# The final token mix of a gated four-layer kernel, taken one batch at a time

## The reference, cut to what matters

```python
# the last attention (8 heads of 4 channels), then the last feed-forward part
x = x + tanh(g_xattn[3]) * L3_xattn(layernorm(x), ctx, ctx, ...)
xn = layernorm(x)
x_prev = concat([zeros, xn[:, :-1]], axis=1)        # the token before
xr = mu_r * xn + (1 - mu_r) * x_prev
xk = mu_k * xn + (1 - mu_k) * x_prev
r = sigmoid(xr @ W_r.T)                             # receptances
k = square(relu(xk @ W_k.T))                        # gates
x = x + tanh(g_ffn[3]) * (r * (k @ W_v.T))          # values
```

## Time and profile before

| what | value |
|---|---|
| time of three executions | 1080.51, 1083.62, 1086.57 us; median 1083.62 |
| the profiled execution | 1080.08 us |
| its span | 1078.3 us, 17505 instructions |
| PE busy | 985.0 us (91% of the span) |
| DVE busy | 776.8 us (72%) |
| ACT busy | 486.8 us (45%) |
| POOL busy | 290.1 us (27%) |

### The profile page before, as it was taken

The page is one execution under the profiler, slowest core; times in us unless marked ns, Lnnn a source line. Parts: engine busy times, 40 slices in busy tenths (PEclk is TensorE's granted clock), DMA queues, the critical chain, the costliest instruction groups (busy, mean ns, idle before and its releaser), DMA issues.

```text
span 1078.3 us, 17505 instructions
## 1 busy us (share of the span) xinstructions
PE 985.0 (91%) x6556; PEld 582.9 (54%) x6556; DVE 776.8 (72%) x1467; ACT 486.8 (45%) x707; POOL 290.1 (27%) x439
## 2 busy tenths in 40 slices
PE   8888975999999977999689999998889999899988
PEld 4323343544444444999254444455678788644445
DVE  5789978999999632454489999985645654799946
ACT  2463341377777710121027777775212212357742
POOL 3556611133343202002313333331300500023320
PEclk9799986999999977999899999999999999899999
DMA  6689921102430333895331233101354242100011
GB/s 204 224 270 292 364 58 65 43 24 89 128 101 24 91 87 112 306 375 187 92 141 54 60 90 87 46 2 41 99 174 137 98 137 82 28 15 18 2 31 39
DMA packets 79181, 121.81 MB, mean 113 GB/s; under 512 B 9733, under 2 KB 52904, under 8 KB 79090
## 3 DMA queue, kind: packets, MB, share of 16 engines
q1 hardware_dynamic: 59278, 79.29, 23.8%
q10 hardware_dynamic: 19044, 39.22, 10.4%
q0 software_dynamic: 768, 2.10, 0.6%
HBM read 92.10 MB, written 27.81 MB: 111 GB/s over the span
## 4 chain that ended last, share of the span: by engine, by line
PE 70%; DVE 21%; issue 4%; ACT 2%; POOL 2%; DMA 1%; SPq 0%; POOLq 0%; DVEq 0%; ACTq 0%
PE bank L1546 14%; PE bank L1512 14%; PE bank L1737 12%; DVE arena L2229 9%; PE st_bank L1667 4%; PE bank L1679 4%; PE st_bank L1531 3%; PE bank L1314 2%; PE st_bank L1737 2%; PE st_bank L1464 1%; PE bank L1584 1%; PE st_bank L1302 1%; PE bank L1565 1%; DVE bnst L1832 1%; DVE arena L1961 1%
## 5 line engine op out<-in xcount | busy, mean ns | idle before, releaser
L2229 DVE TENSOR_REDUCE arena<-bank 128x1 f32<-128x512 f32 x640 | 397.2, 681 | 34.2 <-PE bank L1512 33.2
L1178 ACT ACTIVATE arena<-st_bank 128x1024 f32<-128x1024 f32 x320 | 312.1, 1022 | 136.1 <-PE st_bank L1531 135.0
L1512 PE MATMUL bank<-g_a 64*128 64x512 f32 x480 | 182.3, 480 | 10.7 <-DVE arena L2229 2.5
L1546 PE MATMUL bank<-arena,vaug 128*9 128x256 f32 (+2 forms) x2560 | 168.5, 381 | 2.0 <-ACT arena L1178 2.0
L1512 PEld LDWEIGHTS bank<-g_a 64*128 64x128 f32 x480 | 73.8, 184 | 123.8 <-DVE arena L2229 99.0
L1737 PE MATMUL bank<-g_a,g_w 128*128 128x512 f32 x512 | 117.7, 390 | 4.3 <-DVE g_w L2460 3.2
L1531 PE MATMUL st_bank<-g_a 64*128 64x512 f32 x480 | 115.2, 417 | 0.0
L1737 PEld LDWEIGHTS bank<-g_a,g_w 128*128 128x128 f32 x512 | 95.8, 188 | 25.5 <-DVE g_w L2460 3.6
L901 POOL COPY arena<-arena 8x32 f32<-8x32 f32 x160 | 34.7, 217 | 257.9 <-issue 137.1
L1546 PEld LDWEIGHTS bank<-arena,vaug 128*9 128x9 f32 (+2 forms) x2560 | 55.8, 92 | 75.7 <-issue 39.1
L1512 PE MATMUL bank<-g_x,g_a 64*128 64x512 f32 x160 | 63.1, 497 | 9.6 <-DVE arena L2229 3.5
(11 more groups left out here) (321 smaller groups left out, 1491.1 us busy)
## 6 DMA issues: line engine op xcount, KB each, us to landing
arena<-in_glu_w SPq DMA_DIRECT2D x39, 512.0 KB, 3.3
arena<-kv_table SPq DMA_DIRECT2D x11, 1024.0 KB, 7.9
ctxT<-in_glu_w ACTq DMA_DIRECT2D x22, 512.0 KB, 6.0
arena<-in_w SPq DMA_DIRECT2D x20, 512.0 KB, 6.3
kparts<-arena ACTq DMA_DIRECT2D x12, 512.0 KB, 5.2
arena<-in_w ACTq DMA_DIRECT2D x12, 512.0 KB, 3.6
xnT<-kv_table SPq DMA_DIRECT2D x5, 1024.0 KB, 7.7
g_a<-kparts SPq DMA_DIRECT2D x24, 192.0 KB
```

What stands on the lines that cost most here:

```text
L1178: act.activation(prob[sl % PROBS], st_bank[sl % 2][:], ACT.Exp, scale=scale).then_inc(exp_ready, 1)
L1512: pe.matmul(bank[TURN_BANKS[place % 3]], Qc[gi % KQ_BUFS][rows, qt * P:(qt + 1) * P], Kc[gi % KQ_BUFS][rows, half * CH:(half + 1) * CH], s ...
L1546: ins = pe.matmul(bank[7][at:at + dh + 1, 0:D], vaug[l][:, b * KT + 2 * m + i, h0 + hh, :], tiles[:, a], start=(m == 0 and i == 0), stop=( ...
L2229: dve.tensor_reduce(mxh[gi % 2][:, col, hf:hf + 1], bank[TURN_BANKS[place % 3]], AX.X, ALU.max).then_inc(max_red, 1)
```

## The change

- `mix_loads` moves in SP's list from the end to the start of the third layer's attention, behind the first group's shift rows; it waits for the x that this attention starts from. The mix's arrays now begin behind the attention's part of the arena, so that they can be filled meanwhile.
- Slots 60 and 61 get a step `mix tokens` each in place of their dummies: the norm's transposes of batch 0, one chunk to a slot, through the rotation's banks. DVE copies them out, and after the second makes xk of batch 0.
- Around the last value products, the last context and heads stand the gate products of batch 0, in halves: `mix` (first half of a chunk's accumulation) and `mix rest` (second half). ACT makes the scaled part of xr for batch 0 at the first, and clips the gates at each second half; DVE squares them, and after the second makes xr of batch 0.
- Behind the attention PE does receptances of batch 0, half of its values, the norm's transposes of batch 1, the other half of the values, gates, receptances and values of batch 1. The dummies there are gone.
- ACT takes the sigmoid of two tiles at a time, and does for batch 1 the scaling by mu straight from the bank. DVE only adds the shifted part, and for batch 0 multiplies and adds two tiles at a time.

The diff, cut: the same edits of names in lists are left out, and so are the removed lines of the final mix on PE and DVE, which stand in the code above.

```diff
@@ -103,11 +103,12 @@
 WEIGHT_SLOTS = (2, 6)
-LN_HOLDS = {3: 8, 4: 16, 7: 16}
+LN_HOLDS = {3: 8, 4: 16}
+MIX_BANKS = {"r": (0, 1), "v0": (2, 3), "k1": (6, 7), "v1": (4, 5, 2, 3)}
 SECOND_TOKENS_AT, SECOND_BANKS = 3, 2
 GATHERED_HOLDS = 19
 QUERY_HOLDS = {1: 10, 2: 4}
-CTX_HOLD, UNIT_HOLD, MIX_HOLD = 14, 44, 22
+CTX_HOLD, UNIT_HOLD = 14, 44
...
@@ -148,6 +149,9 @@
         last = first + EC[l] + 2
         finish[last] = ("variance", b)
         finish[last + NORMAL_LAG] = ("normalise", b)
+        if l == 3:
+            for c in range(DC):
+                finish[last + NORMAL_LAG + 2 + c] = ("mix tokens", (b, c))
     def turn(kind, *what):
...
+            if sl in finish and finish[sl][0] in ("heads", "out", "mix tokens"):
                 turn(*finish[sl])
             elif sl in finish:
                 steps.append(finish[sl])
...
+    def first_gate(c):
+        turn("mix", c)
+    def second_gate(c):
+        steps.append(("mix rest", *next(step[1:] for step in steps if step[:2] == ("mix", c))))
+    if l == 3:
+        first_gate(0)
+    steps += [("values", NGROUPS[l] - 1, m) for m in range((KT - VALUES_LAG + 1) // 2, KT // 2)]
+    if l == 3:
+        second_gate(0)
+    steps.append(("copy", NGROUPS[l] - 1))
     context(NGROUPS[l] - 1)
-    steps.append(("tokens", 0))
+    if l == 3:
+        first_gate(1)
+    else:
+        steps.append(("tokens", 0))
     for c in range(EC[l]):
         turn("heads", (B - 1, c))
+    if l == 3:
+        second_gate(1)
     for i in range(2):
         turn("out", (B - 1, i))
...
+        r = Region(after_att)
         mwr, mwk, mwv = (r.take([DC, D]) for _ in range(3))
...
@@ -746,6 +767,8 @@
                         keys_load(l, g)
                     queries_load(l, g) if g else first_queries(l)
                 shift_load(l, 0)
+                if l == 3:
+                    mix_loads()
                 for g in range(ng):
                     if g + 1 < ng:
                         shift_load(l, g + 1)
@@ -801,7 +824,7 @@
                     glu_chunk_load(sp, n)
             def mix_loads():
-                sp.wait_ge(x_ready, 7 * NT)
+                sp.wait_ge(x_ready, 6 * NT)
                 for dst, n in ((mwr, "w_r"), (mwk, "w_k"), (mwv, "w_v")):
                     ld(dst, rows(io[n]), fin_ld)
...
@@ -1134,6 +1156,11 @@
                 else:
                     ins = act.activation(qph[k % 2][0][0:n], bank[j][0:n], ACT.Identity, bias=w[l]["bq"][:, j % EC[l]:j % EC[l] + 1])
                 ins.then_inc(qp_hi, 1)
+            def clipped(b, c, gates):
+                act.wait_ge(rk_mm, 4 * b + c + 1)
+                act.activation(kact[:, c, b * CH:(b + 1) * CH], gates, ACT.Relu).then_inc(rk_relu, 1)
...
                         act.activation(pvs[gi % 2], bank[7][:, 0:D], ACT.Copy).then_inc(pv_evac, 1)
+                    elif step[0] == "mix" and step[1] == 0:
+                        act.wait_ge(fin_ld, 16 * 5)
+                        act.wait_ge(xnT_ready, LN_AT[7] * 4 + DC)
+                        for c in range(DC):
+                            act.activation(xr[:, c, 0:CH], xnT[:, c, 0:CH], ACT.Copy, scale=mmu[:, 0, c:c + 1]).then_inc(mix_scaled, 1)
+                    elif step[0] == "mix rest":
+                        _, c, place = step
+                        clipped(0, c, bank[TURN_BANKS[place % 3]])
                     elif step[0] == "tokens" and l == 2:
...
-            ln_evac(7)
-            for i in range(B * DC):
-                h, c = i // DC, i % DC
-                act.wait_ge(rk_mm, i + 1)
-                act.activation(kact[:, c, h * CH:(h + 1) * CH], bank[i], ACT.Relu).then_inc(rk_act, 1)
-            for t in range(NT):
-                act.wait_ge(rk_mm, B * DC + t + 1)
-                act.activation(rv[:, t, :], bank[6 + t % 2][:, 0:D], ACT.Sigmoid).then_inc(rk_act, 1)
+            def receptances(b):
+                for i in range(QT // 2):
+                    t = b * QT + 2 * i
+                    act.wait_ge(rk_mm, 4 * b + DC + i + 1)
+                    act.activation(rv[:, t:t + 2, :].rearrange("p t d -> p (t d)"), bank[MIX_BANKS["r"][i]], ACT.Sigmoid).then_inc(rk_act, 1)
+            act.activation(exp_ready_table[:], onesf[0:1, 0:1], ACT.Sigmoid)
+            receptances(0)
+            for c in range(DC):
+                act.wait_ge(xnT_mm, LN_AT[7] * 4 + DC + c + 1)
+                act.activation(xnT[:, c, CH:2 * CH], bank[SECOND_BANKS + DC + c], ACT.Copy).then_inc(xnT_ready, 1)
+                act.activation(xk[:, c, CH:2 * CH], bank[SECOND_BANKS + DC + c], ACT.Copy, scale=mmu[:, 1, c:c + 1]).then_inc(mix_scaled, 1)
+            for c in range(DC):
+                act.activation(xr[:, c, CH:2 * CH], bank[SECOND_BANKS + DC + c], ACT.Copy, scale=mmu[:, 0, c:c + 1]).then_inc(mix_scaled, 1)
+            for c in range(DC):
+                clipped(1, c, bank[MIX_BANKS["k1"][c]])
+            receptances(1)
...
+                    if kind == "mix":
+                        return rk_relu, what + 1
                     if kind == "out":
                         return x_ready, stage * NT + what[0] * QT + what[1] * 2 + 2
...
                     ins.then_inc(ctxT_mm, 1)
+                def mix_tokens(which, place):
+                    b, c = which
+                    pe.wait_ge(*bank_read(place))
+                    for t in range(b * QT, (b + 1) * QT):
+                        pe.wait_ge(xn_ready, XN0[7] + t + 1)
+                        ins = pe.transpose(bank[TURN_BANKS[place % 3]][:, t % QT * P:(t % QT + 1) * P], xn[:, t, c * P:(c + 1) * P], ident[:])
+                    ins.then_inc(xnT_mm, 1)
+                def first_gate(c, i, place):
+                    pe.wait_ge(mix_ready, DC)
+                    if i == 0:
+                        pe.wait_ge(*bank_read(place))
+                    ins = pe.matmul(bank[TURN_BANKS[place % 3]], mwk[:, i, c * P:(c + 1) * P], xk[:, i, 0:CH], start=(i == 0), stop=(i == DC - 1))
+                    if i == DC - 1:
+                        ins.then_inc(rk_mm, 1)
                 def output(which, place):
...
@@ -1796,31 +1866,39 @@
             attention(3)
...
+            def receptances(b):
+                pe.wait_ge(mix_ready, 4 * b + 2 * DC)
+                for i in range(QT // 2):
+                    if b:
+                        pe.wait_ge(rk_act, i + 1)
+                    for t in range(b * QT + 2 * i, b * QT + 2 * i + 2):
+                        for k in range(DC):
+                            ins = pe.matmul(bank[MIX_BANKS["r"][i]][:, t % 2 * D:(t % 2 + 1) * D], xr[:, k, t * P:(t + 1) * P], mwr[:, k, :], start=(k == 0), stop=(k == DC - 1))
+                    ins.then_inc(rk_mm, 1)
+            def mixed_values(b, i):
+                pe.wait_ge(rk_sq, DC * (b + 1))
+                for t in range(b * QT + 2 * i, b * QT + 2 * i + 2):
+                    mixed_v = bank[MIX_BANKS["v1"][t % QT]][:, 0:D] if b else bank[MIX_BANKS["v0"][i]][:, t % 2 * D:(t % 2 + 1) * D]
+                    for k in range(DC):
+                        ins = pe.matmul(mixed_v, kact[:, k, t * P:(t + 1) * P], mwv[:, k, :], start=(k == 0), stop=(k == DC - 1))
+                    ins.then_inc(fv_mm, 1)
+            receptances(0)
+            mixed_values(0, 0)
+            ln_transposes(7, [1], SECOND_BANKS)
+            mixed_values(0, 1)
+            for i in range(DC):
+                pe.wait_ge(mix_ready, 2 * DC + i + 1)
+                for c in range(DC):
+                    ins = pe.matmul(bank[MIX_BANKS["k1"][c]], mwk[:, i, c * P:(c + 1) * P], xk[:, i, CH:2 * CH], start=(i == 0), stop=(i == DC - 1))
+                    if i == DC - 1:
+                        ins.then_inc(rk_mm, 1)
+            receptances(1)
+            pe.wait_ge(xnT_ready, (LN_AT[7] + 1) * 4)
+            pe.wait_ge(mix_scaled, 3 * DC)
+            for i in range(QT // 2):
+                mixed_values(1, i)
...
                 ch.link(ins)
+            def shifted(i, dst, b, c):
+                lo, hi = b * S, (b + 1) * S
+                dve.scalar_tensor_tensor(dst[:, c, lo + 1:hi], xnT[:, c, lo:hi - 1], mom[:, i, c:c + 1], dst[:, c, lo + 1:hi], ALU.mult, ALU.add).then_inc(mix_ready, 1)
+            def squared(b, c):
+                dve.wait_ge(rk_relu, DC * b + c + 1)
+                ka = kact[:, c, b * CH:(b + 1) * CH]
+                dve.tensor_tensor(ka, ka, ka, ALU.mult).then_inc(rk_sq, 1)
+            def mixed(b, i, tiles):
+                for t in range(b * QT + 2 * i, b * QT + 2 * i + 2, tiles):
+                    dve.wait_ge(fv_mm, t + tiles)
+                    dve.wait_ge(rk_act, 2 * b + i + 1)
+                    mixed_v = bank[MIX_BANKS["v1"][t % QT]][:, 0:D] if b else bank[MIX_BANKS["v0"][i]]
+                    mixed_v = mixed_v.rearrange("p (t d) -> p t d", t=tiles)
+                    ch.link(dve.tensor_tensor(rv[:, t:t + tiles, :], rv[:, t:t + tiles, :], mixed_v, ALU.mult))
```

(72 more changed lines are left out.)

31 lines of the change are left out of this document (3 added, 28 removed).

## The result

Over 20 executions each, the changed kernel takes 1075.81 us (median; 1068.64 to 1085.69) and the kernel before 1083.24 (1077.34 to 1088.50). The ratio is 0.9925, 95% interval 0.9900 to 0.9949: 7.4 us less at the medians. (The ratio leaves out the changed kernel's 1085.69 us, which lies over 1.5% above its fastest execution and counts as slow; the medians are of all 20.) The profiled execution took 1071.18 us, with a span of 1069.4, which is 8.9 less than the earlier trace rows.

A forecast was written before the change was run, and what follows sets the result against it. Bound: three late blocks of fp32 products, started only with both batches normed and mixed. A gain of 13.9 less a delay of 5.6 gives 8.3; 1083.62 - 8.3 = 1075.3 us, range 1070.5 to 1080.5.

The forecast's parts named there:

- The bound: Kernel's end: three equal blocks of fp32 products, 20.6 us, start only when both batches are normed and mixed.
- The waits in the slots: Slots 60 to 63: batch 0's second copy ends 1035.4, a slot 63 dummy waits for it, xk ready 1037.9.
- The delay: Last contexts to output: gates and in-order waits make the output's first add 5.6 us late, 1047.6 for 1041.98.
- Beside the norm: Behind the output add: batch 0's receptances and values run beside batch 1's norm; PE's last product 1066.9 for 1075.16.
- Weights early: SP's queue in the third layer's attention: five early loads are hidden, cost 0; at most 2.6 us without cover.
- Function sets: ScalarE's tail: the sigmoid's 1.28 us set change is hidden; copy and clipping need none, cost 0.
- the upper bound of 2.6 us: ScalarE, batch 1's path: two more set changes of 1.28 us if copy and clipping each needed their own set.
- The clock: Tail from 1036: forecast kept 1.00; rival, one fall costing 1.7 or 3.4 us, gain 6.6 or 4.9, chance 0.12.
- The whole: Whole kernel: 8.3 us less, 1075.3 on the median; a gain of 6.5 to 10 had chance 0.60.

The follow-up runs named there:

- e4: Changed kernel with VectorE's shift of batch 0's xr moved ahead, into the wait for the first clipped gates; tail (batch 0's normalisation to span end) 39.0 us against 40.0.
- e6: Changed kernel with xr's shift first, and last value products and ScalarE's copy ahead of chunk 0's gates and clipping; tail 37.8 us, ratio to kernel before 0.9888.
- e12: Changed kernel unedited, profiled a third time; tail 41.4 us, with a fall of the clock.
- e1: Changed kernel with batch 0's four gate products moved from among the last contexts to behind the last output products; tail 47.1 us.
- e2: Changed kernel with all of batch 0's transposes, mixing and gates behind the last output products, 22 dummies ahead of the gates; tail 50.1 us.
- e5: Changed kernel with only the last value products and ScalarE's copy put ahead of chunk 0's gates and clipping; tail 40.4 us, with a fall of the clock.
- e3: Changed kernel without the dummies in the third layer's attention slots from 55 on; tail 39.95 us.
- e9: e2 with dummies also in the gaps among contexts, heads and output and ahead of the receptances; tail 47.0 us, clock 1.00.
- e7: e1 with dummies in PE's gaps: three each ahead of last context, heads and output, twelve ahead of the receptances; tail 42.2 us, clock 1.00.
- e11: Changed kernel unedited, profiled a second time; tail 40.1 us, clock 1.00.
- e8: e1 with nine dummies among contexts, heads and output, and VectorE's shift of xr ahead of squaring; tail 39.15 us.
- e10: Changed kernel with ten dummies in gaps ahead of first gate product, last context and receptances; tail 40.1 us, 1074.29 us, ratio to kernel before 0.9915.

## Why the prediction was right, point by point

- **The bound.** "The end is set by three blocks of fp32 products ... which start only when both batches are normed and mixed" held. PE is busy 41.66 us of the tail before and 33.92 after, 7.7 less, and the time in which it is idle changed only from 6.8 to 6.1. The 38 dummies behind the attention alone had been busy for 8.5 us. So the real products moved into time that dummies had filled; PE's gaps hardly shrank.
- **The waits in the slots.** Second copy out of the bank to end at 1035.4: 1034.89 + 0.5 = 1035.4. Xk ready 1037.9: 1037.38 + 0.5 = 1037.9. The dummy of slot 63 waited for that copy (0.3 in the list above), as foreseen.
- **The delay.** Last value products expected from 1038.85: 1038.49 + 0.5 = 1039.0. Sums copied by 1041.85: 1042.0. Output first added at 1047.6: 1047.5. The delay predicted as 5.6 us measured 5.5. What of it cost time at the end is less: 1.06 us came back with VectorE's shifts moved (e4), and another 1.2 with chunk 0's gates and clipping moved behind the last value products and their copy (39.0 to e6's 37.8).
- **Beside the norm.** Transposes done at 1054.35: 1054.1. Gates of batch 1 from 1056.55: 1056.2; I had let ScalarE's four evacuations follow each other a little too slowly. The gates took 3.70 in place of 3.45. PE's last product 1066.9: 1066.85. Span 1070.05: 1069.9.
- **Weights early.** The five issues span 946.31 to 948.7. The first pair of shift rows goes out 0.4 earlier than before (945.09 for 945.51), and so does the next (955.73 for 956.1): no cost.
- **Function sets.** There is one change of set in the tail, 1.28 us at 1045.03, hidden as expected; copies and clipping between two sigmoids needed none. So the upper bound of 2.6 us falls away. By the Trainium skill (ScalarE: Activation LUTs, Table sets: the hidden batching unit) copy and relu are in each set, and this trace agrees.
- **The clock.** I gave a single fall 0.12 and priced it at 1.7 or 3.4 us. The profiled execution kept 1.00, as forecast. But the rival is real: e12 fell, at a price of 1.4 us, close to the 1.7 that I had named. One profile of three, and falls in the near kernels e1, e2 and e5, speak for a chance above 0.12; three profiles can't say how far above. The reason I gave, "no gap over 1.2 us, so I think it holds", was wrong as a reason: e12 fell with gaps of 1.0 and 0.8. The rule of the Trainium skill (TensorE: Matmul & The Clock Gate, Part 4: PE-mode transpose), that transposes don't count as a busy PE in the same way as other products, stays undecided. In e1 the stretch of 3.1 us ahead of the outputs holds eight transposes and no other product (PE busy 1.27), and the clock fell 1.5 us behind it; the kernel before has a stretch as long with sixteen (1037.60 to 1040.74, PE busy 1.97) and kept 1.00. That eight more transposes go with a kept clock speaks against the rule. For it speaks that e1 has transposes in slots 60 and 61 where the kernel before has dummies, and that e2 fell 0.7 us into the eight that stand behind its outputs, where the kernel before has dummies too. And e3 kept its clock with fewer dummies still. Where the same program can go either way, single runs don't settle it.
- **The whole.** Forecast was 1075.3 on the median, measured 1075.81. The tail's 8.4 against a forecast of 8.3 is closer than the method deserves: batch 1's gates started 0.3 us earlier than forecast and took 0.25 longer. The medians differ by 7.4, with an interval from 5.5 to 10.8 us (1083.24 times 0.0051 and 0.0100). Falls of the clock in some executions would explain a gain of the medians smaller than that of the tail, but only the profiled ones show a tail, and that is argued.

Where the 8.4 comes from, with the clock held in each step (one profiled execution each, and the shares would differ if the pieces were taken back in another order): order batch by batch 1.4 (48.4 to e9's 47.0); transposes, copies and xk of batch 0 in slots 60 and 61 another 4.8 (to e7's 42.2); gates among the contexts 2.2 (to 40.0). Nearly all of the last is the wait for xr, 0.8 us in place of 2.9; with the shift first, which removes that wait in both orders, the place is worth 0.2 (39.15 against 39.0). In a kernel without dummies for it, the place of the gates may matter for the clock as well: with the gates behind the outputs and no dummies in the gaps it fell twice and the tail was 47.1 (e1), with them among the contexts it fell once in three executions.

## What to carry to other kernels

When work is moved into an engine's gaps, list the gaps that are left and what each of them waits for: here three waits of under 1 us made 2.5 of the 3.1 us in which PE waited. One went by reordering VectorE's list alone (tail 39.0 against 40.0), without moving a product; placing chunk 0's gates behind the last value products, and ScalarE's copy ahead of its clipping, took 1.2 us more (37.8). Read such a change from a common instruction to the end, not by spans: here what came ahead of the tail differed by up to 14.6 us between runs, more than the change brings. And profile a kernel without dummies more than once: a stretch that keeps its clock in one execution may lose it in the next.

## What the runs showed of the hardware

The clock fell to 1.2 GHz with no long idle stretch before it. In e12 PE was busy 2.81 of 3 and then 2.18 of 3 us, with waits of 1.0 and 0.8 us, and the next 3 us were at 0.50; in e11 the same busy times kept 1.00. Falls cost 1.4 us in e12, 1.7 in e5, and 4.9 in e1, where it fell twice. In the four kernels with dummies in the gaps (e7, e8, e9, e10) the clock was 1.00, in one execution each, and ten of them lengthened the tail by 0.1 us or less (40.12 against 40.03 and 40.09). The 22 dummies behind e2's outputs and transposes came too late: they took 6.39 us where the same in e9 took 4.91, as the clock was at 0.53 from 1045 to 1048.
